# Five order tables laid out anew for two interleaved streams of a four-layer kernel

## The reference

```python
x = _layernorm(x + _L0_attn_ref(x, ...))   # sparse attention: 64 local keys and 32 picked by an indexer, 8 heads
x = _layernorm(x + _L0_ffn_ref(x, ...))    # 16 experts, 4 per token, and one shared expert
x = _layernorm(x + _L1_attn_ref(x, ...))   # Mamba: convolution, then a scan over 512 steps with 16 states
x = _layernorm(x + _L1_ffn_ref(x, ...))    # 8 experts, 1 per token, each takes at most 256 tokens
```

## Time and profile before

| | us |
|---|---|
| median of 3 runs | 1278.72 (1274.86 to 1281.36) |
| the profiled execution, its own time | 1282.89 |
| its span, first to last instruction | 1281.1 |
| DVE busy | 1007.2 |
| PE busy | 869.1 |
| mean granted PE clock, share of full | 0.798 |

### The profile page before, as it was taken

How to read it: one execution, slowest core, us unless ns; L and a number is a source line. 1 busy time by engine, 2 the same in 40 slices (tenths; PEclk the granted TensorE clock), 3 DMA queues, 4 the chain that set the end, 5 groups by cost and what they waited for, 6 DMA issues and landing times. The chain is left out here.

```text
span 1281.1 us, 29248 instructions
## 1 busy us (share of the span) xinstructions
PE 869.1 (68%) x11808; PEld 528.0 (41%) x11808; DVE 1007.2 (79%) x2274; ACT 585.0 (46%) x1299; POOL 53.2 (4%) x40
## 2 busy tenths in 40 slices
PE   6676877787767874576766787475786467746655
PEld 3454655665645552343443444252342133223122
DVE  4657788867576575998977668798976899999985
ACT  4464654634344664533422485542464464621210
POOL 0000000000000100000000010000030022000000
PEclk9587988987858785797877898597797698768676
DMA  4202111121013103232110310333500253222310
GB/s 158 67 4 51 40 51 47 42 48 36 10 48 69 51 3 77 67 84 75 50 44 9 73 39 4 108 68 92 112 5 1 77 136 74 66 70 57 100 33 8
DMA packets 85079, 72.20 MB, mean 56 GB/s; under 512 B 24784, under 2 KB 63696, under 8 KB 84752
## 3 DMA queue, kind: packets, MB, share of 16 engines
q1 hardware_dynamic: 84944, 70.34, 21.7%
HBM read 66.51 MB, written 3.80 MB: 55 GB/s over the span
## 5 line engine op out<-in xcount | busy, mean ns | idle before, releaser
L1356 ACT ACTIVATE big<-DEL,Aneg 128x512 f32<-128x512 f32 x128 | 84.9, 714 | 156.0 <-DVE SG L1877 140.7
L1877 DVE TENSOR_TENSOR_SCAN SG<-big 128x512 f32<-128x512 f32 x128 | 154.8, 1250 | 1.8
L818 PE MATMUL bank<-onehot,tparts 128*32 128x256 bf16 x3840 | 133.8, 296 | 27.8 <-DVE onehot L1656 21.0
L818 PEld LDWEIGHTS bank<-onehot,tparts 128*32 128x32 bf16 x3840 | 104.5, 104 | 61.2 <-issue 30.0
L977 PE MATMUL bank<-XP,CO 128*128 128x512 f32 x128 | 83.0, 782 | 39.1 <-DVE XP L1885 39.1
L977 PE MATMUL bank<-CV,CO 128*128 128x512 f32 x128 | 79.5, 752 | 40.0 <-DVE CV L1885 40.0
L1868 DVE TENSOR_TENSOR big<-DU,BC 128x1024 f32<-128x1024 f32 x64 | 78.3, 1224 | 0.4
L1656 DVE TENSOR_SCALAR onehot<-ib,CO 128x1024 bf16<-128x1024 f16 x160 | 71.8, 489 | 7.5 <-PE bank L818 7.0
L853 PE MATMUL bank<-GT,QBD 128*32 128x32 f32 x3072 | 57.8, 208 | 25.6 <-issue 14.3
L1147 ACT ACTIVATE relu_s<-bank,nml 128x192 f32<-128x192 f32 (+1 forms) x128 | 52.9, 426 | 45.1 <-DVE nml L1612 44.9
L1665 DVE TENSOR_TENSOR GT<-bank,rank_turn 128x512 f32<-128x512 f32 x64 | 43.9, 687 | 35.8 <-ACT GT L1206 35.3
(11 more groups left out here) (288 smaller groups left out, 1871.0 us busy)
## 6 DMA issues: line engine op xcount, KB each, us to landing
BC<-bc_rows SPq DMA_DIRECT2D x128, 256.0 KB, 4.5
ib<-idx_rows SPq DMA_DIRECT2D x64, 256.0 KB, 4.4
rows_bounce<-RO SPq DMA_DIRECT2D x256, 8.5 KB
big<-comb_rows SPq DMA_DIRECT2D x16, 256.0 KB, 4.7
big<-comb_rows SPq DMA_DIRECT2D x8, 512.0 KB, 8.4
W<-w SPq DMA_DIRECT2D x1, 2818.0 KB, 15.3
RB<-rows_bounce SPq DMA_DIRECT2D x16, 136.0 KB, 2.2
X<-x SPq DMA_DIRECT2D x4, 256.0 KB, 2.9
```

What stands on the lines that cost most here:

```text
L818: m = mm(own.bank[3 - c % 2][32 * bb:32 * bb + 32, 256 * kind:256 * kind + 256], own.tparts[:, kt, part, 32 * kind:32 * kind + 32], onehot ...
L1356: A(own.dA[:, n % 2, j, :], own.DEL[:, j, :], ACT.Exp, scale=Aneg[:, j, n:n + 1]).then_inc(dA_ok.sem, dA_ok.up(b))
L1877: m = dve.tensor_tensor_scan(own.hs[:, j, :], own.dA[:, n % 2, j, :], own.dBu[:, n % 2, j, :], 0.0, ALU.mult, ALU.add)
```

## The change

Only the five lists of numbers in `ORDER` are other numbers. Each list still sums to the same number of sections (sync 562, tensor 923, scalar 975, gpsimd 522, vector 1028), and each stream gets the same sections in the same order; no instruction, wait, buffer or transfer is added or removed. Where an engine goes from one stream to the other is new. The new list of GpSimd starts 6, 2, 4, 2, 66 where the old one starts 5, 4, 71. A leading 0 in a list lets the second stream begin.

```diff
     "sync": (
-        7, 7, 11, 11, 16, 16, 16, 16, 16, 16, 32, 6, 5, 3, 11, 25, 16, 1, 1, 1, 4, 5, 11, 7, 1, 2, 20, 2, 11,
-        17, 16, 29, 21, 2, 1, 5, 10, 6, 1, 2, 5, 2, 3, 18, 32, 6, 1, 23, 27, 13, 2, 24),
+        7, 7, 11, 11, 16, 16, 16, 16, 16, 16, 21, 1, 1, 5, 10, 28, 23, 1, 9, 7, 1, 1, 15, 7, 1, 2, 20, 17, 27,
+        29, 21, 2, 1, 5, 10, 4, 1, 2, 5, 2, 3, 1, 1, 1, 24, 18, 7, 4, 1, 2, 1, 23, 26, 35, 2, 2),
     "tensor": (
-        2, 2, 1, 1, 1, 2, 2, 4, 5, 1, 4, 1, 4, 1, 6, 1, 2, 3, 2, 3, 1, 3, 1, 2, 2, 4, 1, 3, 2, 3, 2, 2, 6, 1,
...
-        1, 4, 1, 1, 1, 4, 1, 9, 32),
+        0, 1, 2, 3, 1, 1, 3, 4, 4, 1, 2, 2, 3, 2, 10, 2, 2, 3, 1, 3, 1, 1, 1, 3, 1, 4, 2, 2, 3, 2, 2, 2, 6, 1,
...
+        11, 2, 1, 2, 1, 1, 3, 2, 1, 4, 1, 2, 1, 1, 1, 4, 16),
     "scalar": (
...
-        2, 1, 1, 4, 4, 3, 31),
...
+        3, 3),
     "gpsimd": (
-        5, 4, 71, 65, 72, 62, 60, 57, 63, 63),
+        6, 2, 4, 2, 66, 65, 72, 62, 60, 57, 63, 63),
     "vector": (
-        3, 3, 2, 1, 6, 5, 1, 2, 7, 1, 8, 3, 5, 4, 3, 3, 1, 6, 2, 5, 1, 2, 3, 3, 11, 1, 11, 3, 3, 7, 2, 4, 1,
-        1, 1, 9, 1, 1, 2, 2, 7, 1, 6, 1, 5, 2, 3, 1, 6, 1, 1, 2, 1, 7, 1, 1, 1, 5, 1, 4, 1, 7, 3, 3, 7, 2, 19,
-        2, 1, 1, 6, 4, 9, 9, 6, 1, 6, 9, 1, 3, 3, 4, 5, 2, 3, 1, 13, 3, 1, 4, 3, 2, 4, 2, 7, 1, 15, 1, 3, 3,
-        1, 2, 2, 1, 1, 3, 3, 2, 4, 1, 3, 1, 5, 1, 2, 1, 7, 4, 5, 4, 2, 2, 1, 4, 3, 1, 1, 2, 1, 1, 2, 1, 4, 2,
-        3, 1, 1, 3, 8, 1, 2, 2, 7, 2, 1, 4, 1, 1, 6, 11, 4, 1, 15, 1, 2, 3, 1, 5, 8, 5, 6, 1, 7, 2, 3, 2, 1,
-        3, 2, 1, 1, 6, 4, 10, 7, 1, 8, 2, 7, 1, 3, 3, 1, 2, 3, 3, 3, 2, 7, 1, 2, 1, 3, 1, 5, 1, 4, 1, 3, 1, 2,
-        3, 2, 6, 1, 5, 3, 1, 1, 2, 3, 3, 6, 2, 2, 1, 3, 1, 8, 2, 4, 1, 2, 1, 1, 4, 1, 1, 2, 10, 2, 1, 2, 3, 2,
-        1, 1, 4, 2, 1, 1, 1, 1, 5, 2, 2, 2, 1, 1, 1, 7, 1, 1, 1, 1, 1, 1, 1, 2, 1, 2, 4, 7, 3, 1, 8, 3, 1, 1,
-        2, 1, 1, 1, 1, 4, 2, 1, 1, 1, 2, 2, 1, 1, 1, 2, 2, 3, 1, 1, 1, 2, 2, 1, 1, 2, 1, 1, 2, 2, 1, 2, 1, 1,
-        1, 5, 2, 2, 2, 2, 1, 1, 4, 1, 1, 6, 1, 2, 4, 1, 1, 1, 1, 1, 1, 1, 1, 1, 3, 1, 1, 2, 1, 1, 1, 1, 3, 9,
-        2, 2, 2, 1, 1, 1, 1, 1, 51),
+        1, 2, 2, 1, 2, 1, 6, 5, 1, 2, 7, 5, 6, 3, 10, 13, 2, 1, 2, 2, 3, 2, 6, 2, 6, 2, 3, 1, 8, 7, 2, 4, 1,
+        6, 1, 1, 2, 5, 1, 1, 2, 2, 9, 1, 5, 1, 7, 1, 6, 1, 2, 2, 1, 9, 1, 1, 1, 4, 1, 10, 3, 3, 7, 1, 3, 1, 6,
+        1, 9, 1, 1, 2, 7, 10, 5, 1, 2, 1, 2, 17, 6, 1, 2, 2, 5, 4, 4, 2, 4, 1, 6, 1, 2, 1, 1, 1, 5, 1, 2, 4,
+        1, 1, 2, 1, 1, 2, 1, 1, 3, 2, 3, 1, 4, 2, 4, 1, 4, 1, 2, 3, 6, 4, 3, 7, 6, 3, 14, 1, 7, 1, 5, 1, 3, 2,
+        1, 1, 2, 1, 1, 5, 3, 5, 7, 1, 2, 1, 13, 2, 3, 1, 1, 3, 1, 1, 5, 1, 1, 7, 4, 1, 17, 3, 1, 3, 8, 4, 1,
+        1, 5, 2, 3, 1, 2, 1, 4, 1, 1, 4, 1, 6, 3, 6, 1, 2, 2, 1, 8, 2, 4, 1, 4, 1, 7, 2, 1, 1, 2, 3, 1, 2, 2,
+        1, 1, 3, 3, 2, 3, 1, 6, 1, 5, 1, 7, 2, 5, 1, 3, 10, 4, 2, 3, 2, 3, 1, 4, 1, 4, 2, 10, 1, 4, 1, 1, 3,
+        1, 1, 2, 9, 2, 1, 2, 2, 2, 1, 1, 3, 2, 3, 2, 5, 2, 1, 1, 2, 1, 1, 2, 1, 1, 1, 1, 1, 1, 2, 1, 2, 2, 2,
+        2, 1, 1, 1, 4, 3, 3, 2, 3, 2, 1, 2, 1, 6, 3, 2, 1, 1, 1, 1, 1, 1, 3, 2, 1, 2, 4, 2, 1, 1, 2, 1, 1, 2,
+        2, 2, 1, 1, 2, 1, 1, 2, 2, 1, 1, 1, 3, 1, 1, 1, 1, 2, 1, 1, 4, 4, 1, 2, 1, 1, 2, 1, 2, 3, 8, 2, 1, 1,
+        2, 5, 1, 28, 1, 5, 1, 1, 1, 7, 3, 2, 2, 1, 1, 1, 5, 1, 1, 2, 2, 2, 1, 12, 1, 1, 1, 1),
```

## The result

The changed kernel takes 1227.57 us (median of 4 runs, 1223.87 to 1233.81), the kernel before beside it 1276.79 (4 runs, 1272.55 to 1281.36): a ratio of 0.9619, 95% interval 0.9563 to 0.9675. A second measurement gave 1229.74 and 0.9653 (0.9611 to 0.9694). The profiled execution took 1233.81, its span is 1232.0.

What follows compares the result with a forecast made beforehand. No engine is full, so only idle time, mostly DVE's 274 us, can move. End 12, batch 2's experts 2 and middle 3 make 17 us off 1278.7: 1262 us, own range 1254 to 1270, 8-in-10 range 1248 to 1279.

Steps and rivals of the forecast that it cites:

- The end: Batch 3's last stretch: batch 2's held-back work fills DVE's waits there; 12 us off, between 8 and 15.
- the eight waits: DVE's hand-over waits after batch 3's last scan, 13.9 us together: about 1.3 stays uncovered, 12.6 go.
- the worry about a queue on PE: At the end, hand-overs queuing behind the other stream on PE could add 3 us of new waits.
- idle under 5 us: Sign in the profile after: DVE idles under 5 us in the last 45 us.
- The second store: Batch 2's output stored just ahead of batch 3's at the very end: costs 0.7 us, up to 1.4.
- the middle's term: 255 to 900 us: cover for L1846 and an L1665, 8.8 us at face value; 3 taken, 15 either way.
- Batch 2's experts beside batch 1's scan: 900 to 1005 us: scan sections cover the experts' waits, slowed by POOL's products; 2 us off, from -4 to +6.
- No change: Whole kernel: the end gains and the middle gives as much back; 1276 us, chance 0.17.
- slower: Middle: batch 0's experts, brought forward, hold up attention, 25 us lost and 12 won; 1292 us, chance 0.11.
- less of a gain by POOL and the scan: Batch 2's experts: four POOL products exclude the scan, 1.27 us each, term -4; 1268 us, chance 0.11.
- The full gain of the middle: Middle: all of the 8.8 us and as much again from smaller waits; 1247 us, chance 0.15.
- The first 299 us: Start of the kernel, given as the first 255 us: no change, within 3 us.

Runs made afterwards that it cites:

- C: Mark at the start of batch 3's scan (1102 us after, 1140 before); kernel before with the new order only from there on: 1265.95 us, ratio 0.9882.
- A to B: Kernel before with the new order only from 299 us to the merge of batch 2's attention (557 us after, 589 before): 1263.82 us, ratio 0.988.
- B to C: Kernel before with the new order only from the merge of batch 2's attention to the start of batch 3's scan: 1260.28 us, ratio 0.9871.
- first half: Kernel before with the new order only from 299 us until batch 0's experts are done and batch 2's second tile nearly is: 1283.15 us, ratio 1.0027.
- held `rest`: Kernel before with the new order from 299 us only until batch 1's last attention tile is done, batch 0's `rest` at its old place: 1290.4 us, 1.0076.
- second half alone: Kernel before with the new order only from the end of batch 0's experts to 557 us: 1289.73 us, ratio 1.0101.
- the version beyond both: Changed kernel with five vector scan sections pulled ahead of two waits for RB: 1225.85 us, or 1225.57 with RB's load also ahead of BC's.
- the last two versions: Changed kernel with five vector scan sections ahead of two RB waits, without and with RB's load ahead of BC's: 1225.85 and 1225.57 us; changed kernel beside them 1229.74.

## Why the prediction was right in kind and wrong in size

**The end was right**: 12 us forecast, 15 by its own ratio and 11.1 between C and the end of the two traces. L1967 stands twice in the last 45 us, and the scan alone goes at 4.63 us a state, as foretold. Of the eight waits of 13.9 us, 2.7 are left (0.82 before L1891, 1.57 before L1900, 0.34 before L1959), where I said 1.3. L1900's is where the worry about a queue on PE came true: from the end of L1895 to L1900 it now takes 3.8 us, before 2.2. The sign "idle under 5 us" failed: DVE idles 6.1 us of the last 45 before its own last instruction, and 8.9 to the end of the span; before it was 19.1. The second store, counted at 0.7, cost nothing: the span ends 2.7 us after DVE in both kernels.

**The step that failed is the middle's term**, "I take half the face value less a little: 3". Its two parts measured 15 (A to B) and, of the 17 from B to C, about 10 before 900 us; some 25 in all, beyond its bounds of 15 either way. The mechanism in it was wrong, not only the size. I priced two long waits by the work newly put ahead of them. The runs show that this price says little: L1846 shortened by 5 us gave a loss or nothing, since the tile's rows left 3 to 5 us later for it and SP's queue stood behind; and each half of the new order, with the seam that it needs, gave nothing or a loss, where the whole gave 15. What the new order changes is the spacing. DVE's hidden sections of batch 0's experts (L1793, first and last of nine), before and after:

```profile
387.86 0.68 DVE L1793 TENSOR_TENSOR HT<-SG,U 64x512 f32<-64x512 f32 x1
...
457.43 0.69 DVE L1793 TENSOR_TENSOR HT<-SG,SZ 128x512 f32<-128x512 f32 x1 [3.93 <-PE bank L917]
```
```profile
357.16 0.64 DVE L1793 TENSOR_TENSOR HT<-SG,U 64x512 f32<-64x512 f32 x1
...
406.97 0.69 DVE L1793 TENSOR_TENSOR HT<-SG,SZ 128x512 f32<-128x512 f32 x1
```

They took 69.6 us and now take 49.8, start 31 us sooner and end 50 us sooner, so the conv, dt and scan of batch 0 are there in time to cover batch 2's third and fourth tiles. Leave that continuation out (first half, or the held `rest`) and the tiles stand bare. Shown is that the early experts alone, 7 to 10 us ahead by W = 300, are worth nothing without it. That the spacing makes the whole gain, and why the nine end so much sooner in this order, is argued from the traces only: every part that was cut out inside the middle has a run of one stream that neither order has. `rest(0)` starts at 340.8, where I said near 350, and before at 367.

**Is it TensorE's clock?** In the W = 240 to 360 stretch the granted clock rose from a mean of 0.74 to 0.86 (1.0 is the 2.4 GHz level) and PE's busy time fell by 17 us. Against it: the second half alone had PE busy 109.6 us at 0.78 and took 180.7 us; the version beyond both had it busy longer, and took 156.4:

```profile
339.80:496.20 156.40, 112.36 (x1901) 72.26 (x1902) 119.97 (x281) 93.45 (x203) 10.99 (x9) 0.82 0.21 52
```

So the time does not follow PE's busy time: with about the same of it, 109.6 and 112.4 us, the two orders are 24 us apart. A clock that only one of them is granted stays possible as a small part of the gain; no run here sets the clock apart from the order.

**Batch 2's experts beside batch 1's scan**: forecast 2, measured about 6, the upper end of its range. From W = 680 to 760, before and after:

```profile
907.70:1009.20 101.50, 67.46 (x232) 33.34 (x230) 80.19 (x186) 54.91 (x90) 12.63 (x8) 0.82 0.22 54
```
```profile
872.00:967.70 95.70, 65.86 (x214) 34.48 (x214) 80.46 (x155) 49.25 (x79) 15.22 (x8) 0.81 0.23 62
```

The part from B to C alone has 94.5 us there for 79.3 us of DVE work. The price of company that I took from the earlier trace rows is real. In the changed kernel POOL's products from 852 to 1060 are:

```profile
L1433 POOL TENSOR_TENSOR U<-U,big 128x512 f32<-128x512 f32 x10 | 20.0, 2003 | 255.6 <-DMA big<-comb_rows 224.8 <-DVE U L1802 30.9
L1433 POOL TENSOR_TENSOR SZ<-SZ,big 128x512 f32<-128x512 f32 x6 | 11.9, 1985 | 20.9 <-DVE SZ L1802 20.9
```

near 2.0 us as foretold (1.90 in the stretch itself, where it had been 1.58), and the scans' mean over the kernel rose from 1250 to 1275 ns, 3.2 us over 128. But the idle time filled was more than I counted: the waits of DVE that the profile names there fell from 17.1 to 11.6 us, those for POOL from 4.3 to 1.3 and that of L1838 from 2.1 to nothing, while one (L1822, for ACT) grew from 1.5 to 3.6. By the rule of the Trainium skill, "SBUF — State Buffer", section "SBUF: two separate sides", this term would have been a loss of 4 (nearer 5 by the prediction's own figures: 2.1, less four times 1.27, less 2). The trace agrees with the rule that the two engines hold each other up, as far as both take longer side by side, and not that the term is lost: the stretch is 6 us shorter, and DVE's total busy time grew by 0.8 us only.

**The rivals.** No change, and slower: both fall. Of the slower one, batch 0's experts took 36 us for the steps from the third to the ninth, 38.7 before, and DVE idles 59 us from 302 to 600, not over 80: nothing was held up. Of the less of a gain by POOL and the scan, see above. The full gain of the middle, 1247, named the right part, by the wrong reason, and was still 19 us short. The first 299 us moved by 2.4 us in the trace, within the 3 given.

What stays open: which single hand-over sets the pace in the first tiles of the new order, how much of that pace is TensorE's clock, whether the middle is worth 15 or 20 us in the changed kernel, and whether the 4 us of the last two versions are real.

## What to carry to other kernels

Don't price an order table wait by wait: where two streams hide each other, a wait shortened by putting its steps ahead of the other stream's turns into that stream's next one, and here 5 us of it were worth nothing that could be measured. Compare instead how long equal amounts of the busiest engine's work take, stretch by stretch, with both marks away from a large wait (here one mark said 29 us and the next 23), and ask whether the stream that is brought forward also brings the work that covers what comes after. A part of such a change, tested alone, can show a loss for a whole that gains: cut only where the two orders have done the same sections.

## What the runs showed that I had not expected

SP's queue is a resource of its own in an order: 16 small stores took 5.6 us to issue, 8 row loads 5.0, and the load of RB that DVE needed stood 10.6 us behind them, unseen as long as another wait covered it. Of these only the 5.0 can be saved, since the stores are what it reads back. And repeated runs of the kernel before spread from 1269 to 1288 us, 1.5%, so that 4 us stay unresolved with six runs of each kernel.
